# A transformer layer in split fp32: the next batch's x transposed between this batch's projections and split from SBUF

## The reference

```python
        qkv = x @ w_qkv.T + b_qkv
        q, k, v = jnp.split(qkv, 3, axis=-1)
...
        scores = jnp.einsum('bhfc,bhtc->bhft', k, q)
        causal = jnp.triu(jnp.ones((s, s), dtype=bool))
        scores = jnp.where(causal[None, None], scores, MASKED_BIAS)
        attn = jax.nn.softmax(scores, axis=-2)
        vals = jnp.einsum('bhft,bhfc->bhtc', attn, v)
        vals = vals.transpose(0, 2, 1, 3).reshape(b, s, PART)
        out = vals @ w_o.T + b_o
...
    x = x + _layernorm(_L0_attn_ref(_layernorm(x, axis=-1), L0_attn_w_qkv, L0_attn_b_qkv, L0_attn_w_o, L0_attn_b_o), axis=-1)
    x = x + _layernorm(_L0_ffn_ref(_layernorm(x, axis=-1), L0_ffn_W, L0_ffn_b, L0_ffn_A, L0_ffn_B, L0_ffn_gate_w, L0_ffn_gate_b), axis=-1)
```

## Time and profile before

| | |
|---|---|
| median of 3 runs | 1583.13 us (1582.87 to 1585.05) |
| the profiled execution | 1584.81 us, span 1583.0 us |
| PE busy | 1504.8 us (95%), 8032 matmuls |
| DVE, ACT, POOL busy | 976.6 us (62%), 677.5 us (43%), 558.9 us (35%) |
| mean granted TensorE clock | 0.98 |
| attention phase | up to about 926 us |

### The profile page before, as it was taken

One profiled execution on the slowest core, in us unless ns is written; L12 is line 12 of the kernel. 1 busy time (PEld: TensorE's weight loads), 2 busy tenths in 40 slices (PEclk: granted clock), 3 DMA queues, 4 the chain that ended last, 5 costly groups with the idle time before them and its releaser, 6 DMA issues. The chain is left out here.

```text
span 1583.0 us, 24982 instructions
## 1 busy us (share of the span) xinstructions
PE 1504.8 (95%) x8032; PEld 1319.5 (83%) x8032; DVE 976.6 (62%) x2133; ACT 677.5 (43%) x1464; POOL 558.9 (35%) x1099
## 2 busy tenths in 40 slices
PE   7989989989999999899899779999999999999996
PEld 5878878878878888788787669999999999999996
DVE  7475574675665655755754656666666666666663
ACT  5354364454553653653635542333333333333331
POOL 2241431432332332414312353444444444444443
PEclk9999999999999999999999879999999999999998
DMA  6121112012021111120110531211121112221211
GB/s 226 54 54 42 55 40 76 20 36 76 20 53 60 50 40 46 50 71 25 40 36 21 172 134 37 66 64 66 66 66 66 66 66 66 66 66 66 66 61 40
DMA packets 45774, 98.72 MB, mean 62 GB/s; under 512 B 4912, under 2 KB 21296, under 8 KB 45744
## 3 DMA queue, kind: packets, MB, share of 16 engines
q1 hardware_dynamic: 45744, 98.35, 20.1%
HBM read 56.39 MB, written 25.17 MB: 52 GB/s over the span
## 5 line engine op out<-in xcount | busy, mean ns | idle before, releaser
L1312 PE MATMUL ps_f<-wagh,x2Th 128*128 128x364 f32 x768 | 256.5, 334 | 4.4 <-DVE f L1174 2.9
L1312 PE MATMUL ps_f<-wagl,x2Th 128*128 128x364 f32 x768 | 253.8, 330 | 0.0
L1312 PE MATMUL ps_f<-wagh,x2Tl 128*128 128x364 f32 x768 | 253.4, 330 | 0.0
L782 PE MATMUL ps_o<-xTh,wh 128*128 128x512 f32 x504 | 201.2, 399 | 4.8 <-DVE xTl L468 4.8
L782 PE MATMUL ps_o<-xTh,wl 128*128 128x512 f32 x504 | 197.8, 392 | 0.0
L782 PE MATMUL ps_o<-xTl,wh 128*128 128x512 f32 x504 | 197.1, 391 | 0.0
L1312 PEld LDWEIGHTS ps_f<-wagh,x2Th 128*128 128x128 f32 x768 | 145.6, 190 | 7.2 <-issue 5.0
L1312 PEld LDWEIGHTS ps_f<-wagl,x2Th 128*128 128x128 f32 x768 | 145.7, 190 | 1.3
L1312 PEld LDWEIGHTS ps_f<-wagh,x2Tl 128*128 128x128 f32 x768 | 145.5, 189 | 0.0
L392 POOL TENSOR_SCALAR pr<-pr,rden 128x128 f32<-128x128 f32 (+3 forms) x256 | 136.7, 554 | 0.0
L385 POOL TENSOR_TENSOR cw<-wm,cnt 128x4 f32<-128x4 f32 x64 | 12.8, 200 | 346.0 <-ACT pr L668 346.0
(11 more groups left out here) (152 smaller groups left out, 3533.1 us busy)
## 6 DMA issues: line engine op xcount, KB each, us to landing
kst<-kst SPq DMA_DIRECT2D x64, 256.0 KB, 3.6
xt<-in_x SPq DMA_DIRECT2D x32, 512.0 KB, 4.1
out<-outs SPq DMA_DIRECT2D x32, 512.0 KB, 3.1
xs<-in_x SPq DMA_DIRECT2D x31, 512.0 KB, 4.3
valsT<-vt SPq DMA_DIRECT2D x64, 128.0 KB, 2.3
vraw<-valsT SPq DMA_DIRECT2D x32, 256.0 KB, 4.2
raw<-in_wqkvT SPq DMA_DIRECT2D x12, 512.0 KB, 5.3
wag_raw<-in_wagT SPq DMA_DIRECT2D x8, 546.0 KB, 6.5
```

What stands on the lines that cost most here:

```text
L782: last = pe.matmul(ps[:, :], w[:, k, c:c + P], xT[:, k, :], start=(k == 0 and w is wh and xT is xTh), stop=(k == KD - 1 and w is wl), skip ...
L1312: last = pe.matmul(ps_f[:, g, 0:GW], a[:, k, :], w[:, k, cols], start=(k == 0 and a is x2Th and w is wagh), stop=False, skip_group_check=True)
```

## The change

The transposes of the next x leave slots 4 to 6 and stand in slots 2 to 4, in halves of four (`TURNED`: up to three halves (t, g) in a slot: behind the first half projection, behind `transpose_p` 0 and 1, behind the second half projection). ScalarE copies each half from PSUM back to where it was read, unsplit (`x_back`). Since `xTh` and `xTl` are still being read, the split comes in slot 5: the first halves of k after the first half of q3 (`x_read`), the second after the whole (`q_full`). ScalarE and VectorE split tiles 0 and 1 (`x_high`, `x_low`), POOL tiles 2 and 3, both parts (`split_x`), all from SBUF. All projections of k and q but q3 are now halves, one in each place. The one order of `ps_j` gives way to a count for each kind (k_full, k_high, k_low and so on): k has bank 0, q bank 1. Scores 1, 2, 3, 6 and 7 are ahead; those of head 4 come after the first half of k3, with the exponentials later on ScalarE. High and low parts of a slot's first place come later in its order, except in slots 0, 1 and 5.

All four tiles of the next x must now lie in SBUF at once. Tile 3 gets `x3`, which shares its room with `wl_v_late`, the low parts of V's weights for the last two blocks k: they are stored in DRAM once, and loaded again for each batch once x is split.

```diff
     WHOLE, FIRST, SECOND = range(KD), range(KD // 2), range(KD // 2, KD)
     BETWEEN = [
         ([("v", 0, 0, WHOLE), ("v", 1, 0, WHOLE)], []),
         ([("v", 2, 0, WHOLE)], [("v", 3, 0, WHOLE)]),
-        ([("k", 2, 0, WHOLE)], [("q", 2, 0, FIRST)]),
-        ([("q", 2, 0, SECOND)], [("k", 3, 0, WHOLE)]),
-        ([("q", 3, 0, WHOLE)], [("x", 0, 1, WHOLE)]),
-        ([("x", 1, 1, WHOLE)], [("x", 2, 1, WHOLE)]),
-        ([("x", 3, 1, WHOLE)], [("k", 0, 1, WHOLE)]),
-        ([("q", 0, 1, FIRST)], [("q", 0, 1, SECOND), ("k", 1, 1, FIRST)]),
+        ([("k", 2, 0, FIRST)], [("k", 2, 0, SECOND)]),
+        ([("q", 2, 0, FIRST)], [("q", 2, 0, SECOND)]),
+        ([("k", 3, 0, FIRST)], [("k", 3, 0, SECOND)]),
+        ([("q", 3, 0, FIRST), ("q", 3, 0, SECOND)], [("k", 0, 1, FIRST)]),
+        ([("k", 0, 1, SECOND)], [("q", 0, 1, FIRST)]),
+        ([("q", 0, 1, SECOND)], [("k", 1, 1, FIRST)]),
         ([("k", 1, 1, SECOND)], [("q", 1, 1, FIRST)]),
         ([("q", 1, 1, SECOND)], []),
     ]
     BETWEEN_LAST = BETWEEN[:2] + [([(kind, p, 0, FIRST)], [(kind, p, 0, SECOND)])
                                   for kind, p in (("k", 2), ("q", 2), ("k", 3), ("q", 3))] + 4 * [([], [])]
+    TURNED = {2: [(0, 0), None, (0, 1)], 3: [(1, 0), (1, 1), (2, 0)], 4: [(2, 1), (3, 0), (3, 1)]}
+    X_SLOT = 5
     BARE = 6
+    AHEAD = (1, 2, 3, 6, 7)
+    BEHIND = 4
+    SOON = (0, 1, 5)
     SLOTS = len(BETWEEN)
-    AHEAD = (3, 4, 5, 6)
-    EARLY = [("x", t, g) for t in range(NT) for g in range(2)] + [("k", 0), ("q", 0), ("k", 1), ("q", 1)]
-    NOW = [("v", 0), ("v", 1), ("v", 2), ("v", 3), ("k", 2), ("q", 2), ("k", 3), ("q", 3)]
+    KEPT = KD - 2
...
         wh = sb("wh", [P, KD, E], F32R)
-        wl = sb("wl", [P, KD, E], F32R)
+        wl = sb("wl", [P, KD, 2 * PART], F32R)
+        wl_v = sb("wl_v", [P, KEPT, PART], F32R)
+        with ExitStack() as shared:
+            x3 = sb("x3", [P, 2, PART], F32, shared)
+        wl_v_late = sb("wl_v_late", [P, KD - KEPT, PART], F32R)
         xTh = sb("xTh", [P, KD, S], F32R)
         xTl = sb("xTl", [P, KD, S], F32R)
...
-                    sp.wait_ge(j_lo, j_index(("x", 3, 1), b) + 1)
+                    sp.wait_ge(k_full, 4 * b + 1)
                     for t in range(3):
                         load_x(t, b + 1)
                 for h in range(SLOTS):
+                    if h == 2 and not last:
+                        sp.wait_ge(v_full, 4 * b + 4)
+                        load_x(3, b + 1)
+                    if h in (3, 5):
+                        dup_k((h + 1) // 2, b)
+                    if h in (7, 9) and not last:
+                        dup_k((h - 7) // 2, b + 1)
                     if h >= 2:
                         store_vals(h - 2, b)
-                    if h in (2, 4):
-                        dup_k(h // 2 + 1, b)
-                    if h == 4 and not last:
-                        sp.wait_ge(j_full[1], j_uses(("x", 0, 1), b + 1))
-                        load_x(3, b + 1)
-                    if h in (7, 8) and not last:
-                        dup_k(h - 7, b + 1)
+                    if h == 6 and not last:
+                        sp.wait_ge(x_lo_pool, 4 * b + 8)
+                        sp.dma_start(wl_v_late[:, :, :].bitcast(F32), wl_late[:, :, :]).then_inc(wl_back, 16)
...
+            sp.wait_ge(w_ready, len(W_CHUNKS))
+            sp.dma_start(wl_late[:, :, :], wl_v_late[:, :, :].bitcast(F32)).then_inc(wl_back, 16)
...
+            def split_x(g, b):
+                if g == 0:
+                    pool.wait_ge(x_read, b)
+                else:
+                    pool.wait_ge(q_full, 4 * b)
+                for t in (2, 3):
+                    n = 4 * b + 2 * g + t - 5
+                    pool.wait_ge(x_raw, 8 * b - 7 + 2 * t + g)
+                    pool.tensor_tensor(hold[:, 2 + 2 * g + t:3 + 2 * g + t], mone[0:1, :], mone[0:1, :], ALU.mult)
+                    pool.tensor_scalar(x_place(xTh, t, g), x_turned(t, b, g), 1.0, 1.0, ALU.mult, ALU.mult)\
+                        .then_inc(x_hi_pool, 1)
+                    pool.wait_ge(x_hi_pool, n)
+                    pool.tensor_tensor(x_place(xTl, t, g), x_turned(t, b, g), x_place(xTh, t, g).bitcast(F32),
+                                       ALU.subtract).then_inc(x_lo_pool, 1)
             def body(b, last):
                 for h in range(NH):
-                    if h == 5 and not last:
-                        layernorm(3, b + 1)
+                    if h == X_SLOT and not last:
+                        split_x(0, b + 1)
+                        split_x(1, b + 1)
                     normalise(h, b)
-                    if h < 3 and not last:
+                    if h < 4 and not last:
                         layernorm(h, b + 1)
...
+            def x_low(g, b):
+                for t in range(2):
+                    dve.wait_ge(x_hi_act, 4 * b + 2 * g + t - 3)
+                    dve.tensor_tensor(x_place(xTl, t, g), x_turned(t, b, g), x_place(xTh, t, g).bitcast(F32),
+                                      ALU.subtract).then_inc(x_lo_dve, 1)
...
             def body(b, last):
                 for h in range(SLOTS):
                     if h < NH:
                         scores_max(h, b)
-                    lows(h, 0, b, last)
+                    if h == X_SLOT and not last:
+                        x_low(0, b + 1)
+                    if h in SOON:
+                        lows(h, 0, b, last)
+                    if h == X_SLOT and not last:
+                        x_low(1, b + 1)
                     if last and h == 9:
                         first_attention_out()
-                    if h == 5 and not last:
-                        layernorm_stats(3, b + 1)
                     if h >= 2:
...
                     if h < NH:
                         reciprocal(h, b)
+                    if h not in SOON:
+                        lows(h, 0, b, last)
                     lows(h, 1, b, last)
...
+            def x_back(t, g, b):
+                act.wait_ge(x_full, 8 * b - 7 + 2 * t + g)
+                act.activation(x_half(t, b, g), ps_j[X_BANK[t, g]][:, :], ACT.Copy).then_inc(x_raw, 1)
+            def x_high(g, b):
+                if g == 0:
+                    act.wait_ge(x_read, b)
+                else:
+                    act.wait_ge(q_full, 4 * b)
+                for t in range(2):
+                    act.activation(x_place(xTh, t, g), x_turned(t, b, g), ACT.Copy).then_inc(x_hi_act, 1)
...
             def body(b, last):
                 for h in range(SLOTS):
-                    bare = last and h >= BARE
-                    highs(h, 0, b, last, "x")
-                    if h < NH and not bare:
+                    late = h == BEHIND or last and h >= BARE
+                    if h == X_SLOT and not last:
+                        x_high(0, b + 1)
+                    backs(h, 0, b, last)
+                    if h < NH and not late:
                         exps(h, b)
-                    highs(h, 0, b, last, "qkv")
+                    if h in SOON:
+                        highs(h, 0, b, last)
+                    if h == X_SLOT and not last:
+                        x_high(1, b + 1)
                     if h >= 2:
                         vals_lo_part(h - 2, b)
                     if 1 <= h <= NH:
                         for g in range(2):
                             p_hi(h - 1, g, b)
-                    if h < NH and bare:
+                    backs(h, 1, b, last)
+                    if h < NH and late:
                         exps(h, b)
+                    if h not in SOON:
+                        highs(h, 0, b, last)
+                    backs(h, 2, b, last)
                     highs(h, 1, b, last)
                     if last and h == NH:
                         for n in POOL_SPLITS:
...
+            def transpose_x(t, g, b):
                 pe.wait_ge(xn_ready, 4 * b + t + 1)
-                for g in range(2):
-                    if not (isinstance(b, int) and b == 0):
-                        bank_free(("x", t, g), b)
-                    elif t >= 2:
-                        pe.wait_ge(j_lo, 2 * t + g - 3)
-                    for k in range(4):
-                        last = pe.transpose(x_bank(t, g, b)[:, k * P:(k + 1) * P],
-                                            at[:, (4 * g + k) * P:(4 * g + k + 1) * P], ident[:, :])
-                    last.then_inc(j_full[g], 1)
-            def project(kind, p, b, ks):
-                bank = j_bank((kind, p))
-                ps = pair_bank(kind, p, b)
-                if 0 in ks and ps is ps_j[bank]:
-                    bank_free((kind, p), b)
+                if (t, g) == (0, 0):
+                    pe.wait_ge(v_low, 4 * b)
+                elif (t, g) == (1, 0):
+                    pe.wait_ge(k_low, 4 * b - 1)
+                elif (t, g) == (2, 1):
+                    pe.wait_ge(q_low, 4 * b - 1)
+                else:
+                    pe.wait_ge(x_raw, 8 * b - 8 + 2 * t + g)
```

(93 more changed lines are left out.)

211 lines of the change are left out of this document (114 added, 97 removed).

## The result

**The change makes the kernel slower.** The median is 1596.72 us (1594.81 to 1598.9, 4 runs) against 1583.0 us (1581.96 to 1585.05, 4 runs) of the kernel before: a ratio of 1.0086, with an interval of 1.0065 to 1.0106. The forecast was 1562 us, its range ended at 1577.

What follows compares the result with a forecast made beforehand. TensorE was taken to lose 7.2 us a batch in slots 4 to 6. New waits of 4.9 left -16.1 over 7 batches; with -2.9 and -2.5, -21.5 from 1584.8: 1563.3, median 1562 us, range 1545 to 1577.

Steps and rivals of the forecast that it cites:

- The walk of waits: Waits left or new in TensorE's looped batch, summed place by place: 4.9 us a batch in place of 7.2.
- x(2,0): Slot 3, transposes of the next x's tile 2, first half: TensorE waits 2.5 us for ScalarE's preceding copy of x.
- k0's first half for POOL: First half projection of the next batch's k, pair 0: waits 0.4 us for POOL's split of x.
- k3's first half: First half projection of k, pair 3: waits 0.45 us for the copy that frees the PSUM bank it shares.
- Clock: Batch 0's fall of TensorE to 1.2 GHz taken as gone: -2.5 us; other end 0, or more falls.
- Rival B: Clock drops and copies queued behind exponentials take back everything, another 2.3 us a batch: 1577 to 1586; chance 0.08.
- These 7.2 us go: Slots 4 to 6: 7.2 us a batch lost beside the pieces' prices, all removed by projections between the transposes.
- Head 4's chain: From head 4's exponentials to its last transposes of P: 16.7 us against TensorE's 16.1, a wait of 0.9.
- The last batch: Last batch: k3's first half fills the wait before head 4's scores, once, for -2.9 us.
- C: POOL's split becomes the bound at the next batch's k0 halves: 17 us slower, 1600; chance 0.07.
- A: The new waits, above all slot 3's, are hidden by slack in VectorE's order: 55.8 us go, 1527; chance 0.10.
- D: The DRAM store or reload of V's low weights delays V's first product, 3 us a batch: 1583; chance 0.03.

Runs made afterwards that it cites:

- both repairs: Changed kernel, with head 3's exponentials behind ScalarE's copy of x and VectorE's second subtractions of x behind the values' sum and P's low parts: 1551.92 us.

## Why the prediction was wrong

At the start of the last batch the changed kernel stands at 830.62, where the prediction's terms put it at 815.11 - 16.1 - 2.5 = 796.5: 34.1 too late. From there on it was 2.6 us better than forecast, which leaves 31.5, the distance of 1563.3 from 1594.8.

- **The walk of waits was right in sum, and that was partly luck.** Forecast 4.9 us a batch, measured 4.78, too little at one place and too much at the four others: at x(2,0) 2.14 for 2.5; at head 4's last transposes 2.19 for 0.9; at the spread matmuls 0.32 and else almost nothing for 0.6; k0's first half for POOL 0.13 for 0.4; k3's first half 0 for 0.45, since matmuls at 1.2 GHz hid it (it is 0.3 in the first batch, which has no fall there). x(2,0), POOL's tile (2.1 us for 2.2) and its half (5.1 for 5.4) were sound.
- **The step that failed is "Clock".** It set a fall as gone, -2.5, because waits of 4.9 us spread over 50 us seemed milder than 7.2 in 19. The runs show the opposite. Two single waits of 2.1 and 2.2 brought two falls a batch, 3.04 us. Over seven batches, the first with one fall, that is 20 us, where the forecast had none. The trace of before held a sign of it, in the very batch that the term was taken from. The prediction calls batch 0's waits the same as those of the steady one; they are not:

```profile
114.92 0.69 PE L837 MATMUL ps_t<-ident,pr 128*128 128x128 f32 x2 [1.75 <-DVE PTl L474]
```

```profile
111.80 1.29 DVE L459 BATCH_NORM_STATS2 stats<-xs 128x6 f32<-128x512 f32 x2 [1.36 <-DMA xs<-in_x]
```

In batch 0 VectorE's statistics of tile 3 waited 1.36 us for the tile's load, and TensorE then waited 1.75 us for P's low parts, where it waits 0.67 in the other batches. The 6.8 us at 1.2 GHz begin within this wait, at 114.4. Of the 2.47 us that batch 0 is longer, 0.50 are waits and 1.97 TensorE's longer busy time. In the other six batches no wait is over 1.0 us, and one of them has a fall. Rival B named this, gave it 8 in a hundred, and 2.3 us a batch for falls and queued copies together; the argument against it, "the waits are shorter than today's", counted their sum and not the longest one.
- **"These 7.2 us go" was too much by 2.2.** They were worked out as the stretch's 19.41 us less pieces at the price of their best rows. With the waits nearly gone, TensorE's work in a batch is 104.92 us, not 109.90 - 7.2 = 102.7. Only 4.1 of the 7.2 was idle time (19.41 - 15.31); the rest was taken for idle because a piece took longer than its best case. Pieces do so after the change too: the 16 halves of k and q take 2.82 us on average in the batch with both repairs, from the first matmul to the next piece, where the earlier trace rows gave 2.71 and the same work took 2.77 before. Against 2.71 that is 0.11 a half. Only 0.8 us a batch of TensorE's busy time went with the waits (105.74 - 104.92), of the 3.1 that the prediction counted as lost beside the idle time; which pieces keep the rest was not taken apart. Seven batches: 15.5 us.
- **Head 4's chain was too short by 1.3**, most of it because the loss was charged to one side. The prediction took POOL's loss beside VectorE's subtractions from the earlier trace rows, and gave VectorE 0.3. Without POOL's split the wait is 0.96, where the prediction's walk without this 0.3 gives 16.7 - 16.1 = 0.6; the other 1.23 us is VectorE held up. The Trainium skill (SBUF — State Buffer, section SBUF: two separate sides) lets whichever of the two began first keep the shared ports for its whole instruction. The traces are near it: VectorE's first pair lost 1.85 - 1.29 = 0.56 beside a scaling of POOL's of 0.61, its second 1.48 beside a scaling of 0.61 and a subtraction of 1.61. The prediction used that rule against POOL alone.
- **The last batch**: -2.9 forecast, 1 to 4 us measured alone. Right.
- Of the rivals, C gave the nearest number, 1600, by a mechanism that did not occur: k0's halves hardly wait for POOL. A would have needed the waits hidden. D left no mark: no wait of V's first product for the borrowed room shows in any looped batch.

The reckoning over the seven looped batches, with the kernel of both repairs as the measure of work without a fall: work 2.2 us a batch more than taken (15.5), TensorE's longer busy time in falls (19.8), waits a little less than forecast (-0.3), and -0.8 for the fall that the kernel before had in its fifth batch, which the forecast had left in: 34.2 for the 34.1. Without the falls the change would have won next to nothing: a looped batch of 112.7 - 3.0 = 109.7 against 109.9.

## What to carry to other kernels

When short waits are merged into fewer, longer ones, look at the longest single wait and not only at the sum. Here the first wait of 2.1 us, taken away with its fall, gave back 3.3 us a batch (112.74 to 109.41); the 4.16 us of before, in pieces of at most 1 us, went with a fall in few batches. When work moves to POOL from and into SBUF, charge VectorE too, and look at what stands behind its two-operand subtractions; here moving one pair behind three instructions and one set of exponentials behind a copy turned a loss of 0.9% into a gain of 2%. And take idle time from the idle column, not from the difference to best-case prices.

## What the runs showed of the hardware

- A fall to 1.2 GHz lasted 3.4 us in the looped batches of every kernel here, but for one of 6.8 us in the first batch of before. One of 3.4 us added 1.2 to 1.5 us to TensorE's busy time. Where short waits stood behind it, part of this was hidden: the fifth batch of before was busy 1.3 us longer and lasted 0.8 us longer than its neighbours. It came behind waits of 2.1 to 2.2 us in 4 to 7 batches of seven, behind 0.9 and 1.5 in one of seven: behind P's last transposes every time, behind x(2,0) not. Why that differs at nearly the same length of wait stays open; no run tells it.
- VectorE and POOL lose to each other instruction by instruction: 1.29 became 2.77 for a pair of VectorE's, 0.18 became 0.71 for POOL's smallest.
- From the start of the last batch to the end of the kernel, two profiles of the one kernel with both repairs differed by 3.2 us.
